# Gated delta net block, two products of the recurrence: 128-column matmuls on half the array, or 64-column matmuls on its quarters

## The reference, cut to what matters

```python
def step(S, inp):                      # S: 64 x 128 for each batch and head
    q_t, k_t, v_t, a_t, b_t = inp
    kS = jnp.einsum('bhd,bhdv->bhv', k_t, S)
    kkS = jnp.einsum('bhd,bhv->bhdv', k_t, kS)
    S = a_t[..., None, None] * (S - b_t[..., None, None] * kkS) + jnp.einsum('bhd,bhv->bhdv', k_t, v_t)
    o_t = jnp.einsum('bhdv,bhd->bhv', S, q_t)
    return (S, o_t)
...
o = _rms_norm(o).astype(x.dtype).reshape(Bx, Tx, H * DV)
return o @ Wo.T
```

## Time and profile before

| | |
|---|---|
| median of 3 runs | 4922.19 us (4921.31 to 4924.02) |
| the profiled execution | 4922.06 us, span 4920.1 us |
| PE busy | 4354.5 us (89% of the span), 59788 matmul instructions |
| PEld busy | 3200.6 us (65%) |
| DVE busy | 3584.4 us (73%) |
| ACT busy | 2863.4 us (58%) |
| POOL busy | 1311.9 us (27%) |
| L585, 4096 matmul instructions | 431.8 us busy, mean 274 ns |
| L588, 4096 matmul instructions | 429.3 us busy, mean 272 ns |

### The profile page before, as it was taken

One profiled execution on the slowest core, in us unless ns is written; L12 is line 12 of the kernel. 1 busy time (PEld: TensorE's weight loads), 2 busy tenths in 40 slices (PEclk: granted clock), 3 DMA queues, 4 the chain that ended last, 5 costly groups with the idle time before them and its releaser, 6 DMA issues. The chain is left out here.

```text
span 4920.1 us, 155226 instructions
## 1 busy us (share of the span) xinstructions
PE 4354.5 (89%) x59788; PEld 3200.6 (65%) x59788; DVE 3584.4 (73%) x8216; ACT 2863.4 (58%) x4519; POOL 1311.9 (27%) x1318
## 2 busy tenths in 40 slices
PE   5999999999999999999899999989999998999955
PEld 4666666666666666666666666666666666666644
DVE  6777777777777777777777777777777777777745
ACT  2555656565565656555565655556565655656533
POOL 2222222222222222222222222222222222222211
PEclk9999999999999999999999999999999999999977
DMA  1111111111111111111111111111111111111111
GB/s 51 43 38 41 36 38 40 36 41 38 41 36 39 39 36 41 38 41 36 42 36 36 41 38 41 36 42 36 36 40 38 41 37 41 36 36 40 36 36 42
DMA packets 873889, 191.75 MB, mean 39 GB/s; under 512 B 811904, under 2 KB 869504, under 8 KB 873856
## 3 DMA queue, kind: packets, MB, share of 16 engines
q1 hardware_dynamic: 867552, 173.48, 16.7%
q0 software_dynamic: 6304, 17.84, 1.3%
HBM read 136.16 MB, written 55.06 MB: 39 GB/s over the span
## 5 line engine op out<-in xcount | busy, mean ns | idle before, releaser
L803 DVE SCALAR_TENSOR_TENSOR cv<-ps,w_v,cv 128x512 f32<-128x512 f32 x768 | 576.7, 751 | 382.3 <-ACT cv L669 364.2
L803 DVE SCALAR_TENSOR_TENSOR cv<-ps,w_kq,cv 128x512 f32<-128x512 f32 x768 | 574.3, 748 | 85.7 <-ACT cv L669 67.6
L525 PEld LDWEIGHTS ps<-Z,NM 64*64 64x64 f32 x8192 | 263.0, 135 | 330.2 <-issue 330.2
L585 PE MATMUL ps<-QG,S 64*128 64x64 f32 x4096 | 431.8, 274 | 4.1
L588 PE MATMUL ps<-PT,U 64*128 64x64 f32 x4096 | 429.3, 272 | 0.0
L978 POOL TENSOR_TENSOR qn<-sl,sq 128x512 f32<-128x512 f32 x128 | 161.9, 1265 | 980.6 <-ACT sq L707 980.6
L445 PE MATMUL ps<-Lm,k_all 128*128 128x512 f32 x768 | 418.4, 626 | 0.0
L525 PE MATMUL ps<-Z,NM 64*64 64x64 f32 x8192 | 294.3, 221 | 132.3 <-DVE accT L915 132.3
L669 ACT ACTIVATE cv<-ps,w_kq 128x512 f32<-128x512 f32 x256 | 175.9, 687 | 398.4 <-PE ps L434 398.4
L585 PEld LDWEIGHTS ps<-QG,S 64*128 64x128 f32 x4096 | 342.6, 188 | 31.4 <-issue 31.4
L963 POOL COPY stP<-tabP 128x24 f32 (+1 forms) x128 | 25.3, 197 | 1220.0 <-DVE KT L832 1213.0
(11 more groups left out here) (177 smaller groups left out, 10306.6 us busy)
## 6 DMA issues: line engine op xcount, KB each, us to landing
scrN<-Nd SPq DMA_DIRECT2D x256, 128.0 KB, 2.4
Z<-scrZ SPq DMA_DIRECT2D x256, 128.0 KB, 2.8
X<-scrX SPq DMA_DIRECT2D x256, 128.0 KB, 3.0
w_v<-wtab SPq DMA_DIRECT2D x128, 132.0 KB, 2.5
w_kq<-wtab POOLq DMA_DIRECT2D x128, 132.0 KB, 2.4
wo_s<-wo SPq DMA_DIRECT2D x128, 128.0 KB, 2.4
NS<-scrN SPq DMA_DIRECT2D x128, 64.0 KB, 2.5
scrZ<-XT SPq DMA_DIRECT2D x128, 64.0 KB, 2.5
```

Source lines behind the costliest of these rows:

```text
L525: last = nc.tensor.matmul(sub_block(ps, 2 * 512, b, a, z), sub_block(BD["NM"], 0, b, a, z), sub_block(BD["Z"], 0, b, a, z), start=True, st ...
L585: nc.tensor.matmul(o_cols(h, b), unit(S, b)[a:z], sub_block(BD["QG"], 0, b, a, z), start=True, stop=False)
L803: nc.vector.scalar_tensor_tensor(cv4[:, j], pj[:, :, k:k + C], tap(j, k), cv4[:, j], ALU.mult, ALU.add).then_inc(conv.sem, 1)
```

## The change

Each matmul call of `pe_o` becomes two calls. The first takes value columns 0 to 63 of the block of S or U and writes output partitions 0 to 63; the second takes columns 64 to 127 and writes partitions 64 to 127 of the same bank. The four calls for one batch and one operand thus use the four 64 x 64 quarters of the array: rows 0 to 63 with either half of the columns, then rows 64 to 127 with either half. The moving operand (64 columns of `QG` or `PT`) is streamed once for each half, where it was streamed once. The number of calls goes from 32 to 64 in a step. The waits, the sums and the values are the same, and nothing else is edited.

```diff
--- before.py
+++ after.py
@@ -570,9 +570,9 @@
                                                 start=True, stop=True)
                 last.then_inc(u_mm.sem, 1)
 
-        def o_cols(h, b):
-
-            return ps[:, (4 + h) * 512 + b * C:(4 + h) * 512 + (b + 1) * C]
+        def o_cols(h, b, d):
+
+            return ps[d:d + 64, (4 + h) * 512 + b * C:(4 + h) * 512 + (b + 1) * C]
 
         def pe_o(pe, m):
             pe.wait_ge(qg_ok.sem, qg_ok.at(m))
@@ -582,11 +582,13 @@
                 pe.sem_inc(pe_go.sem, 1)
                 for b in GROUPS[g]:
                     for h, (a, z) in enumerate(HALF):
-                        nc.tensor.matmul(o_cols(h, b), unit(S, b)[a:z], sub_block(BD["QG"], 0, b, a, z),
-                                         start=True, stop=False)
+                        for d in (0, 64):
+                            nc.tensor.matmul(o_cols(h, b, d), S[a:z, b * P + d:b * P + d + 64], sub_block(BD["QG"], 0, b, a, z),
+                                             start=True, stop=False)
                     for h, (a, z) in enumerate(HALF):
-                        last = nc.tensor.matmul(o_cols(h, b), unit(U, b)[a:z], sub_block(BD["PT"], 0, b, a, z),
-                                                start=False, stop=True)
+                        for d in (0, 64):
+                            last = nc.tensor.matmul(o_cols(h, b, d), U[a:z, b * P + d:b * P + d + 64], sub_block(BD["PT"], 0, b, a, z),
+                                                    start=False, stop=True)
             last.then_inc(o_mm.sem, 2)
 
         def pe_ds(pe, m):
```

## The result

The changed kernel takes **4990.41 us** (median of 4 runs, 4989.73 to 4991.71) against 4921.94 before: a ratio of 1.0139, 95% interval 1.0121 to 1.0156, 68.5 us **slower**. The forecast of no change was wrong and the time lies 0.4 us over the range.

The account below looks back on a forecast made before the run. VectorE was taken to bound the step from the outputs' stage to line 525; the stage's +0.05 us would be absorbed, 0 to 6 us in all, taken as 0, giving 4922 us, range 4900 to 4990.

Parts of the forecast that it names:

- What bounds the kernel: From the outputs' stage to line 525 VectorE sets the step; stage savings or costs go first into the pause before line 487.
- The stage, +0.05 us: Outputs' stage: 64 calls at 0.058 us take 3.77 us against 3.72 before, +0.05 us per step.
- the bound below: Outputs' stage with all four quarters at work: a call costs half of 0.058 us, the stage 1.9 us.
- My rule: Outputs' stage: second half of a call overlaps only the first half of the next, so four quarters give 0.058 us per call.
- The bound above: Outputs' stage, halves sharing rows not overlapping: 5.6 to 7.4 us; as rival +170 to +400 us, chance 0.11.
- the second rival: All four quarters work at once: stage about 1.9 us, longer pause before line 487, more half-clock stretches, 4962 us; chance 0.09.
- The pauses stay, so do the half-clock stretches: 0 us: Pauses before lines 487 and 496 stay, half-clock steps stay one in three; path +0.00 to 0.05 us per step, taken as 0.
- The third rival: Half-clock stretches become rarer through shorter pauses or fuller array use: up to 44 us faster, 4878 us; chance 0.08.

Follow-up runs that it names:

- e6: Kernel before plus eight patterns of 16 dummy calls behind the Gram product: 0.117 us per call on one quarter, 0.058 on two; whole-kernel time says nothing.
- e1: Changed kernel with the two inner loops of the outputs' stage swapped, so calls alternate between row halves: 4990.98 us, ratio 1.0143.
- e4: Kernel before with 16 unread dummy calls per step in TensorE's pause before line 487: 4875.38 us, ratio 0.9906.
- e12: e10 with 16 dummy calls per step before line 487: 4593.29 us, ratio 0.9332.
- e10: Changed kernel with GpSimd's NM product moved ahead of qn and QG into the next pass behind the key product, no dummy calls: 4704.92 us, ratio 0.9561.

## Why the prediction was wrong, point by point

**What bounds the kernel.** Right for the kernel before: the time from the outputs' stage to line 525 is VectorE's, and what the stage saves goes into the pause before line 487 (saved 1.83, pause +1.94). In the changed kernel TensorE's half-clock work comes into that path, by the tap for which VectorE now waits in every step.

**The stage, +0.05 us: this step failed.** It was -1.83. I priced a call right (0.058 on the diagonal) and the bound below right (0.029, 1.9 us), but took the wrong end. The step was the reading of line 598's first loads: the second call's load, 0.05 us behind the first on an idle quarter, made me conclude that a waiting second half of a call holds up the calls behind it. The row itself does not bear out that the second load waits: the first call's two loads, both for one quarter, last 0.14 us together, hardly more than one of them (0.13), so the second began within 0.01 us of the first. e6 shows that a waiting half does not hold up the calls behind it: one quarter throughout takes 0.117 per call, any two 0.058, and four in turn 0.03, even with four instructions in a row on each. My rule gives 0.058 for four, since it allows an overlap only between calls next to each other in the order. Why line 598's second call begins 0.05 late is not settled; e1 took away one reading of it, that a call on other rows must wait. The first loads on an empty array were the weaker evidence: two hypotheses gave the same rate for two quarters, and I let a start-up detail decide between them for four.

**The bound above**, halves that share rows do not overlap: refused, as line 323 said. The Trainium skill, TensorEngine Tiling (Array Packing), Key Properties, which the second rival drew on, says that different tiles can load weights and multiply in parallel; L628 and the 0.0295 us per call of the changed kernel agree.

**The pauses stay, so do the half-clock stretches: 0 us.** This fell with the stage. The second rival had the whole chain: stage 1.9 us (1.89), pause 3.3 (3.43), nothing faster, stretches more frequent, +20 to +83 us (+68.5). I gave it 0.09 and 4962 us; the clock's part of it was 54 us, from every step instead of one in three. The upper end of my range came from this rival, so that the time lies only 0.4 us over it says nothing for the forecast.

**What I had nowhere:** the 15 us of VectorE's operations standing still behind GpSimd. I wrote that QG "is 0.15 later and needed a step later" and looked at who needs QG, not at what VectorE does while GpSimd computes it. The two operations of 1.1 us among their like of 0.2 were in the trace of before (2477.63 and 2479.13).

**The third rival**, fewer stretches and 44 us less, is what e4 did on purpose: -46.

## What to carry to other kernels

Work taken from an engine ahead of a wait that another engine ends only lengthens the wait. On TensorE the longer wait here also cost the clock of what comes behind it: 1.8 us saved per step became 0.54 us lost. Before pricing such a saving, look for what ends the wait and price that: the same change made the kernel 212 us faster once VectorE's chain was shorter, and 277 us faster with the pauses filled as well. In a chain of small operations, compare each one's length with its like: those five times as long were held by another engine.

## What the runs showed of the hardware that I had not expected

- Four 64 x 64 quarters of the array work at once in float32: 0.0295 us per call with 64 columns loaded and 64 moving, against 0.058 on two and 0.117 on one. Halves that share their rows overlap like any others (L628). The Trainium skill, TensorE: Matmul & The Clock Gate, Part 3, says that a weight load overlaps running matmuls only when the row group differs. This trace does not agree: in L628 weight loads begin within 0.01 us of a matmul's start on the same rows, and a call takes 0.058 us there as it does where the rows differ (L631), against 0.117 on one quarter.
- TensorE's granted clock fell to half behind these pauses: before, 1.49 us and 0.62 us with one product of 1.15 us between them, in one step of three; in the changed kernel 3.43 us alone in two steps of three, and 3.43 and 0.60 us around that product in the others. Useless matmuls in that place bring 46 us (e4) and, in e12, 112 us.
- VectorE's 0.16 to 0.17 us operations on SBUF take 1.1 us while GpSimd multiplies, and end with its product; the convolutions, which read one operand from PSUM, are not stretched by GpSimd's Lm product beside them (0.75 us each with it and without). The Trainium skill, GPSIMD Engine Reference, Specifications, names this sharing of SBUF interfaces (VectorE operations with two SBUF inputs or in a mode of two ports). The operation of 64x18, with two inputs in SBUF, agrees: 1.13 us before, 0.17 in e10. The one of 64x2 has one input and stood as well, 1.08 against 0.16; in which mode it ran, no run here shows.
